# Three edits to a Mamba-2 layer with a 4-bit feed-forward gate: order of the last body, order of the feed-forward stage, place of the sums of squares

## The reference

```python
xn = _layernorm(x, axis=-1)
s = _L0_attn_ref(xn, ...)                    # Mamba-2 mixer
g = _silu(_L0_ffn_ref(xn, ...))              # 4-bit feed-forward
return x + s * g
# mixer: proj = xn @ in_proj_w.T -> gate, xBC, dt; causal conv (4 taps) and silu on xBC -> x, B, C
#   chunked scan, 128 heads of 64, 8 groups, chunks of 128 tokens:
scores = jnp.einsum('bclhn,bcshn->bchls', Cc, Bc) * Lmat
Ydiag = jnp.einsum('bchls,bcshp->bclhp', scores, xdt)
Yoff = jnp.einsum('bclhn,bchpn,bchl->bclhp', Cc, prev, jnp.exp(cs))
Y = (Ydiag + Yoff).reshape(Bsz, S, H, P) + x * D[None, None, :, None]
#   yg = Y * silu(gate); per group of 1024 channels:
rstd = jax.lax.rsqrt(jnp.mean(jnp.square(yg_g), axis=-1, keepdims=True) + EPS)
out = (yg_g * rstd).reshape(Bsz, S, INTER) * norm_w
return out @ out_proj_w.T
# feed-forward, W1, W3 (1376 x 512) and W2 (512 x 1376) unpacked from nibbles times scales:
h = jax.nn.silu(a) * b
return jnp.einsum('bsh,dh->bsd', h, W2)
```

## Time and profile before

| what | value |
|---|---|
| time, median of 3 | 1822.46 us (1822.26 to 1824.16) |
| profiled execution: device time | 1824.03 us |
| profiled execution: span | 1822.2 us |
| TensorE busy | 1779.2 us, 98% of the span |
| VectorE, GpSimd, ScalarE busy | 78%, 70%, 67% |
| share of the chain that ended last | PE 86%, POOL 4%, DVE 4%, issue 3%, DMA 2% |
| mean granted TensorE clock | 0.995 |

### The profile page before, as it was taken

The page is one execution under the profiler, slowest core; times in us unless marked ns, Lnnn a source line. Parts: engine busy times, 40 slices in busy tenths (PEclk is TensorE's granted clock), DMA queues, the critical chain, the costliest instruction groups (busy, mean ns, idle before and its releaser), DMA issues.

```text
span 1822.2 us, 30186 instructions
## 1 busy us (share of the span) xinstructions
PE 1779.2 (98%) x10292; PEld 1460.2 (80%) x10292; DVE 1424.7 (78%) x2196; ACT 1226.1 (67%) x2450; POOL 1273.5 (70%) x880
## 2 busy tenths in 40 slices
PE   6899999999999999999999999999999999989998
PEld 5688888888888888888888888888888888867777
DVE  7877888888878888788788888878878878858840
ACT  4877777767776777777767777677777786633320
POOL 4478777767877787777776787778777777656641
PEclk9999999999999999999999999999999999999999
DMA  4433243333323343333333342333333333234422
GB/s 158 171 117 105 92 128 118 92 105 117 122 92 113 102 123 105 105 101 118 120 100 102 111 131 92 106 109 116 103 105 107 118 113 99 92 102 140 138 84 92
DMA packets 122466, 203.35 MB, mean 112 GB/s; under 512 B 22800, under 2 KB 60048, under 8 KB 122064
## 3 DMA queue, kind: packets, MB, share of 16 engines
q1 hardware_dynamic: 120592, 197.71, 34.6%
q10 hardware_dynamic: 1728, 3.78, 0.5%
HBM read 194.09 MB, written 7.34 MB: 111 GB/s over the span
## 4 chain that ended last, share of the span: by engine, by line
PE 86%; POOL 4%; DVE 4%; issue 3%; DMA 2%; ACT 1%; SPq 0%; POOLq 0%; ACTq 0%; DVEq 0%
PE bank L130 14%; PE bank L132 14%; PE bank L131 14%; PE bank L495 11%; PE bank L534 7%; PE bank L582 6%; PE bank L584 6%; PE bank L583 6%; PE bank L630 3%; PE bank L739 3%; DMA q_s<-w3s_dram 1%; POOL up_lo L1436 1%; POOL conv_lo L1386 1%; PE bank L605 1%; DVE q_raw L1298 1%
## 5 line engine op out<-in xcount | busy, mean ns | idle before, releaser
L1377 POOL TENSOR_TENSOR yt<-yt,ec 128x384 f32<-128x384 f32 x128 | 175.1, 1368 | 348.7 <-DVE ec L1111 348.7
L1047 DVE SCALAR_TENSOR_TENSOR z<-bank,cw_all,z 128x511 f32<-128x511 f32 (+2 forms) x477 | 356.1, 747 | 11.3
L812 ACT ACTIVATE lm<-lm,hp 128x128 f32<-128x128 f32 x1024 | 313.1, 390 | 0.8
L1102 DVE TENSOR_TENSOR xdt<-bank,hp 128x512 f32<-128x512 f32 x128 | 88.3, 690 | 231.4 <-PE bank L630 230.3
L130 PE MATMUL bank<-xn_hi,conv_hi 128*128 128x512 f32 x640 | 262.0, 409 | 5.3 <-DVE z L1047 5.3
L1081 DVE SCALAR_TENSOR_TENSOR lm<-lm,gm 128x1024 f32<-128x1024 f32 x128 | 261.3, 2042 | 2.8 <-ACT lm L812 2.8
L132 PE MATMUL bank<-xn_hi,conv_lo 128*128 128x512 f32 x640 | 251.6, 393 | 0.0
L131 PE MATMUL bank<-xn_lo,conv_hi 128*128 128x512 f32 x640 | 250.5, 391 | 0.0
L1381 POOL TENSOR_TENSOR yt<-yt,gate 128x512 f32<-128x512 f32 x128 | 228.0, 1782 | 19.3 <-POOL yt L1377 1.4
L1386 POOL TENSOR_TENSOR conv_lo<-raw_x,conv_hi 128x512 fp32r<-128x512 f32 x124 | 219.5, 1771 | 6.5 <-ACT conv_hi L752 6.5
L851 ACT ACTIVATE z<-bank,cw_all 128x512 f32<-128x512 f32 x128 | 99.1, 774 | 170.1 <-PE bank L132 170.1
(11 more groups left out here) (136 smaller groups left out, 3925.8 us busy)
## 6 DMA issues: line engine op xcount, KB each, us to landing
lm<-cs_d SPq DMA_DIRECT2D x128, 512.0 KB, 4.0
raw_x<-w_conv_dram SPq DMA_DIRECT2D x128, 256.0 KB, 3.0
ec<-e_d SPq DMA_DIRECT2D x256, 96.0 KB, 3.7
raw_g<-w_gate_dram SPq DMA_DIRECT2D x64, 256.0 KB, 2.7
raw_o<-w_out_dram SPq DMA_DIRECT2D x64, 256.0 KB, 2.7
raw_b<-w_conv_dram SPq DMA_DIRECT2D x32, 256.0 KB, 3.2
q_raw<-w1q_dram SPq DMA_DIRECT2D x10, 256.0 KB, 3.3
q_s<-w1s_dram SPq DMA_DIRECT2D x10, 256.0 KB, 3.5
```

Source lines behind the costliest of these rows:

```text
L812: e = act.activation(lm[m % 3][:, u, :], lm[m % 3][:, u, :], ACT.Exp, bias=hp[bd.seq][:, Q_CS, k1, u:u + 1])
L1047: dve.scalar_tensor_tensor(dst[:, d:SEQ], src[:, 0:SEQ - d], cw_all[:, bd.group, pos, 3 - d:4 - d], dst[:, d:SEQ], ALU.mult, ALU.add).then ...
```

## The change

What it does:

- **Sums of squares.** The block at k = 0 leaves `extra` for a new `sum_squares`, called after `turn_x`. So the transposes come first and the wait for `sqa_done` after them, at every k = 0 from body 1 on. In the drain nothing changes place, since `turn_x` has no work there.
- **Last body on TensorE.** In step 5 `gate_mm` comes before `y_diag`. In steps 6 and 7 the order is `out_mm`, `y_diag`, `up`, then `turn_x`, where it was `y_diag`, `out_mm`, `turn_x`, `up`.
- **Drain on the other engines.** `unpack(1, 1, P, UP)` moves ahead of the drain step k = 1 on VectorE and ScalarE, and ahead of k = 2 on GpSimd.
- **Feed-forward stage.** ScalarE's silus of tile m - 1 move from behind to ahead of its DOWN rounding (`silus_up`, `early`).
- **End.** The addition of x moves from GpSimd to VectorE, as a `scalar_tensor_tensor` behind the product.

The change was described as touching a hand-ordered prologue too; the diff has no edit there, and the prologue is the same on both sides.

```diff
@@ over_bodies @@
-def over_bodies(eng, step, ahead, begin=None):
+def over_bodies(eng, step, ahead=None, begin=None, drain=None):
...
     for k in range(3):
+        if drain:
+            drain(k)
         step(DRAIN, k)
@@ TensorE @@
+            def sum_squares(body, k):
+                before = body.plus(-1)
+                if k == 0 and before.exists():
... (the block that stood in extra, unchanged)
             def step(body, k):
                 y_off(body, k)
                 conv(body, k)
-                y_diag(body, k)
-                gate_mm(body, k)
-                out_mm(body, k)
+                if body.is_number(BODIES - 1) and k == 5:
+                    gate_mm(body, k)
+                    y_diag(body, k)
+                    out_mm(body, k)
+                elif body.is_number(BODIES - 1) and k in (6, 7):
+                    out_mm(body, k)
+                    y_diag(body, k)
+                    if k == 6:
+                        pe.wait_ge(taps_x, 3 * TILES * BODIES)
+                    else:
+                        pe.wait_ge(gev_done, TILES * BODIES)
+                    up(0, 0, P, 0, k - 6)
+                else:
+                    y_diag(body, k)
+                    gate_mm(body, k)
+                    out_mm(body, k)
                 extra(body, k)
                 turn_x(body, k)
+                sum_squares(body, k)
@@ ScalarE, VectorE (k == 1) and GpSimd (k == 2) @@
-            unpack(1, 1, P, UP)
+            def drain(k):
+                if k == 1:
+                    unpack(1, 1, P, UP)
@@ ScalarE @@
-            def hidden(m, k, rows):
+            def silus_up(m, k, rows):
                 for b in range(SEQS):
                     act.wait_ge(up_done, 2 * m + b + 1)
                     wait(act, fm_done, 2 * m + b - 1)
                     act.activation(fa[0:rows, b, :], bank[4 * k + 2 * b][0:rows, :], ACT.Silu).then_inc(fs_done, 1)
+
+            def hidden(m, k, rows):
...
-            staggered(act, unpack, hidden)
+            staggered(act, unpack, hidden, silus_up)
@@ VectorE, output tiles @@
+                dve.wait_ge(r1_done, t + 1)
+                dve.scalar_tensor_tensor(fh[:, t % 2, :], fh[:, t % 2, :], 1.0, q_s[t % 2][:, :], ALU.mult, ALU.add
+                                         ).then_inc(r2_done, 1)
@@ GpSimd, output tiles @@
-            for t in range(TT):
-                pool.wait_ge(r1_done, t + 1)
-                pool.tensor_tensor(fh[:, t % 2, :], fh[:, t % 2, :], q_s[t % 2][:, :], ALU.add).then_inc(r2_done, 1)
@@ staggered @@
             unpack(i * 2 + k, k, P, UP)
+            if early:
+                early(i * 2 + (k - 1), 1 - k, P)
             unpack(i * 2 + (k - 1), 1 - k, P, DOWN)
             hidden(i * 2 + (k - 1), 1 - k, P)
     unpack(MT, MT % 2, MREST, UP)
+    if early:
+        early(MT - 1, (MT - 1) % 2, P)
     unpack(MT - 1, (MT - 1) % 2, P, DOWN)
     hidden(MT - 1, (MT - 1) % 2, P)
+    if early:
+        early(MT, MT % 2, MREST)
     unpack(MT, MT % 2, MREST, DOWN)
     hidden(MT, MT % 2, MREST)
```

## The result

| what | before | after |
|---|---|---|
| time, median of 4 runs each | 1822.93 us (1822.26 to 1824.16) | 1811.24 us (1810.84 to 1813.24) |
| profiled execution, device time | 1824.03 us | 1811.29 us |
| profiled execution, span | 1822.2 us | 1809.5 us |
| TensorE busy | 1779.2 us | 1772.8 us |
| mean granted TensorE clock | 0.995 | 0.998 |

The ratio is 0.9938 (95% interval 0.9926 to 0.9950), which is 11.7 us less (9.1 to 13.5). Forecast were 1808.9 us, in a range of 1805.0 to 1814.5, and 13.6 us less. The time lies in the range, but the sum behind it was not right in every term.

What follows compares the result with a forecast made beforehand. The prediction took TensorE to bound nearly everything. Its terms 3.0 (sums), 5.6 (last body and seam), 4.4 (feed-forward with clock) and 0.6 (end) made 13.6 us, from 1822.46 to 1808.9 us, range 1805.0 to 1814.5.

Steps and rivals of the forecast that it cites:

- What bounds the kernel: Whole kernel: TensorE bounds nearly everything, so the edits are worth only what they take from its path.
- Part 1: Sums behind the transposes at k = 0: 0.43 us of TensorE's wait for `sq_sum` saved seven times, 3.0 us.
- nothing is won: Odd bodies at k = 0: nothing waited there, so the new order gains nothing and costs nothing.
- Part 2: Last body: `gate_mm` or `out_mm` covers the waits for `ec`, `y_lo` is late next; drain's `y_off` 1.5 us earlier.
- Part 3: Seam: unpacking in the drain, 0.9 us of contention; tile 1 at 1635.6 instead of 1641.24, 5.6 us with Part 2.
- Part 4: Seam: without the 4.94 us wait the clock should stay up in tile 1, worth 2.2 us.
- Part 5: Feed-forward tiles: moved silus cut the tile from 11.62 to about 11.0 us; stage 111.2, gain 4.4 with the clock.
- I put 0.5 us of wait there: Tile 2's start in the feed-forward stage: its loads, behind the accumulator's 1 MB store, cost 0.5 us of wait.
- the rival that has the load bind the tile: Feed-forward tiles: L1298 stays contended, loop stays 11.62 us, Part 5 gives 0; total gain 9.2, 1813.3 us; chance 0.20.
- Part 6: Last output tile: the addition of x is shorter on VectorE, 0.69 us for GpSimd's 1.26; gain 0.6 us.
- The slower rival (ScalarE in lockstep): Feed-forward tiles: VectorE's DOWN part falls behind the silus, each tile one chain of 13.6 us; 1831 us; chance 0.03.

Runs made afterwards that it cites:

- e5: Kernel before with only tile 1's unpacking moved into the drain, TensorE's order as before: 1820.37 us against 1822.93, ratio 0.9990.
- e2: Kernel before with the last body's new TensorE order and tile 1's unpacking within the drain: 1818.49 us, ratio 0.9976.
- e6: Kernel after, with SyncE asking for tile 2's w1 and w3 before it waits for and stores the accumulator: 1811.23 us, ratio 0.9932 to the kernel before.
- e1: Kernel before with only the sums of squares moved behind the transposes: 1820.21 us against 1822.88, ratio 0.9985.
- e4: Kernel before with only the end's addition of x moved to VectorE: 1821.54 us, ratio 0.9991.
- e8: Kernel after with both SyncE edits, tile 2's loads ahead of the store and packed weights asked for early: 1808.94 us, ratio 0.9923 to the kernel before.
- e3: Kernel before with only ScalarE's silus moved ahead of its DOWN rounding: 1819.59 us, ratio 0.9983.
- e9: e8 with VectorE's two nibble operations on 64 partitions made one on 128: 1807.37 us against 1822.28 for the kernel before, ratio 0.9920.
- e7: Kernel after, with w1's and w3's packed weights asked for once VectorE has read the buffer: 1811.14 us, ratio 0.9937 to the kernel before.
- e10: e8 with GpSimd making `y_lo` ahead of `sq_sum` in the last body's last steps: 1810.73 us, ratio 0.9931 to the kernel before.
- e11: Kernel after with the edits of e8, e9 and e10 together: 1805.09 us, ratio 0.9906 to the kernel before.

## Why the prediction was right or wrong

**What bounds the kernel:** right. Every gain but the 0.6 at the end was time in which TensorE stood idle or ran at the lower clock, and the parts add up to within about 1 us.

**Part 1, 3.0 forecast, 2.4 measured.** The mechanism was right in the even bodies, where 0.40 of 0.43 was won. The step that failed is "nothing is won" in the odd ones: there each order has its own cost, and the new one takes 0.05 more, in eight bodies. I had one row of each kind and looked at one kind. Together with 0.03 per even body it is the missing 0.6.

**Part 2, 1.5 forecast.** The drain's `y_off` came 6.86 us earlier (1622.74 to 1615.88), of which 5.35 is the prologue (2.91) and part 1 (2.44), so 1.5, right in size. e5 against e2 gives 1.4. The waits were not where I put them: I had `out_mm` of step 7 wait for `y_lo`, and the waits stand in step 6 (1.15) and in the drain (0.78, 0.31). Step 6 had become late enough, it seems, that step 7 found its `y_lo` ready. The sum hit the size, not the path.

**Part 3, with part 2 5.6 forecast, 5.63 measured (e2).** Right. From `y_off` to the last sums it takes 7.22 us (1615.88 to 1623.10), before 6.65: 0.57 of contention and waits where I had taken 0.9. By the Trainium skill (SBUF — State Buffer, Who interferes with whom), whichever of the two engines comes second to the shared ports blocks until the other is done. The drain's rows agree that both can be the one that waits: VectorE's nibble operations take up to 1.40 there for 0.42, and GpSimd's last `y_lo` 1.72, which took 1.26 before. The bounds of this part were added up 0.2 us wrongly: 1635.6 less 0.9 is 1634.7, and with 2.2 in place of 0.9 it is 1636.9; that changes no reading here.

**Part 4, clock 2.2.** No step of 0.42 after the seam, granted clock 1.00 in both stretches: right as an event. But as time it isn't there: the wait for tile 2's loads takes the same place in tile 1, 13.11 us against 13.14.

**Part 5, 4.4 forecast with the clock, 1.1 measured.** This is the step that failed. The 3.2 us that are missing have two terms. The first is the start: "I put 0.5 us of wait there" was 2.16 over a tile of 10.95, and was 1.66 short. I had seen that the loads stand behind the store, but not priced it: two pairs of loads and their unpacking take from 1631.28 to 1643.37, 12.1 us, while TensorE needs 10.9. In the kernel before the low clock, which made tile 1 two microseconds longer, had covered just this. e2 shows it without the silus, e6 takes it away, and e1 and e4 show the cover at work: there the low clock made tile 1 13.86 and 13.78 us long, the next two tiles took 10.88, and the stage was 115.5 and 115.6 as before. The second is the steady tile: 11.0 was 11.19 and in two tiles 11.84 and 11.43, together 1.6. I also had 10.95 for TensorE's own tile, which is 10.88 where nothing is waited for. Here I was nearly right on the length of VectorE's loop, since VectorE without its waits for data would need 11.19 - 1.02 = 10.2, my 10.3. What the working lacked is that VectorE's durations aren't fixed: they were read where half of them stood alone. When the loads come earlier (e8), the same operations stand beside GpSimd's and the loop is 11.2 again. So even the rival that has the load bind the tile was only half of it; it forecast 0 for part 5, and e3 gives 3.1 for the silus by themselves.

**Part 6, 0.6 forecast, 0.6 measured.** Right, with 0.69 for the addition.

**The sum.** Forecast 13.6, in the traces 9.8: 0.6 in part 1 and 3.2 in part 5. The median lies only 2.3 above the forecast, 0.5 of which is the base (1822.93 for 1822.46 with a fourth run), because the medians differ by 11.7; 9.8 lies in their interval as well. The hit is in part luck. The slower rival (ScalarE in lockstep) didn't show: no tile passes 11.84 but the first.

## What to carry to other kernels

When a stall is removed, ask what had been hidden in it: here tile 1's low clock covered a chain of loads that was too long by 2 us, and 2.2 us of the seam's gain went there until the loads were moved too. A loop over engines that contend has no fixed length; read each operation's short and its long duration, and expect that more of them are long once the engine no longer waits (10.3 us added up here, 11.2 measured in e8). Fewer, wider operations on the engine that pays (one of 128 partitions for two of 64) gave 0.3 us in each tile where earlier data gave nothing more.

## What the runs showed of the hardware

**Contention costs both engines.** In the feed-forward stage most of it falls on VectorE: a nibble operation takes 0.42 alone and 1.40 beside a GpSimd operation, a 128 x 512 one 0.69 alone and 1.66, while GpSimd's of 1.29 go to 1.75 at most. In the bodies GpSimd pays as well: its 128 products `yt<-yt,gate` in the kernel before take 1.28 at least, 2.08 in the median and 2.11 at most; in the drain, with VectorE idle, it is 1.30 (at 1625.40). VectorE's operations that read one operand from a PSUM bank aren't stretched by it (`fh<-bank,fa` 0.67 to 0.69 in all tiles of the kernel after). A nibble operation on 128 partitions takes 1.5 beside GpSimd (3.10 for two in e9), hardly more than one on 64 (1.40). I had expected a milder price for VectorE.

**The same prologue differs by 3 us.** Up to body 1 the code is the same in all kernels, and the stretch took 167.65 us in one profiled execution and up to 171.33 in others (e3). Kernels with the old order took 168.4 to 171.3 and those with the new one 167.7 to 170.9. TensorE's first wait, for x, was 12.43 us before and 10.97 after, and the mean clock of the first 84 us was 0.95 and 0.98; e6 had 12.3 and 0.98 and took 170.9, so the clock alone doesn't explain it. That is as much as most single parts here are worth, so stretches must be compared from a common mark, and few runs can't order kernels 1 us apart.

**A queue that issues slowly.** SyncE's issue of w1's scales takes 1.27 us behind the store (1632.02) and mostly 0.54 to 0.60 elsewhere, and the data was used 5.6 us after the issue began there; in the steady tile it is 3.5 (1689.51 to 1692.98). The store isn't the only case: the issue at 1655.40 in the kernel after takes 1.89 with no store near it, and the tile in which it falls is the one of 11.84. What slows an issue there isn't shown.

**The same stall did and didn't bring the clock down.** Behind the wait of 1.8 to 1.9 us at tile 2 the granted clock fell to 0.50 for 3.4 us in e2 and e5, and held in the kernel after and in e7. In e10 two waits of 0.5 to 0.6 us were followed by 3.4 us at the lower level; in e11 with one of them, and in e9 with waits of 0.68, 1.54 and 0.55 in the last body and the drain, the clock held. So a stall of this size puts some 1.6 us at risk, and its length alone doesn't say whether they are lost.
